# The norms' row of a random-feature layer goes through DRAM, and the first copies and the last blocks' steps are set anew

## The reference, cut to what matters

```python
def _rfs(xw, ab, AB, gs):
    dot_products = jnp.einsum('...d,rd->...r', xw, ab[:, None] * gs)
    correction = (0.5 * jnp.sum(xw * xw, axis=-1))[..., None] * (ab * ab)
    return 1.0 / math.sqrt(NUM_RFS) * AB * jnp.exp(dot_products - correction)
...
xn = _layernorm(x, axis=-1)
s = jnp.einsum('bsr,or->bso', _rfs(xn, ab, AB, proj), _rfs(input_weights, ab, AB, proj))
h = silu(tlin(xn, w1_w, w1_s)) * tlin(xn, w2_w, w2_s)
h = gelu(tlin(h, h1_w, h1_s))
h = gelu(tlin(h, h2_w, h2_s))
x = x + s * silu(tlin(h, w3_w, w3_s))
```

## Time and profile before

| | |
|---|---|
| median of 3 runs | 1345.27 us (1344.98 to 1350.56) |
| the profiled execution | 1345.51 us, of which the span from the first to the last instruction 1343.7 us |
| TensorE busy | 1320.0 us, 98% |
| mean granted TensorE clock | 0.997 |
| DMA moved | 193.85 MB, 144 GB/s on the mean |

### The profile page before, as it was taken

One profiled execution on the slowest core, in us unless ns is written; L12 is line 12 of the kernel. 1 busy time (PEld: TensorE's weight loads), 2 busy tenths in 40 slices (PEclk: granted clock), 3 DMA queues, 4 the chain that ended last, 5 costly groups with the idle time before them and its releaser, 6 DMA issues.

```text
span 1343.7 us, 16732 instructions
## 1 busy us (share of the span) xinstructions
PE 1320.0 (98%) x6428; PEld 1119.5 (83%) x6428; DVE 946.5 (70%) x1205; ACT 766.2 (57%) x1036; POOL 589.1 (44%) x596
## 2 busy tenths in 40 slices
PE   7989999999999999999999999999999999999997
PEld 6867898888988889888888888888898888988887
DVE  7767867778677786678865776656767567665665
ACT  5546655566555664466654666546565565655564
POOL 4556988999899998888880000000000000000000
PEclk9999999999999999999999999999999999999999
DMA  9798432545324552254521444224432244313351
GB/s 360 290 358 304 147 103 96 170 152 174 103 96 149 176 162 90 94 177 156 178 98 63 134 149 141 79 73 147 154 113 79 94 152 133 109 63 120 132 165 40
DMA packets 88372, 193.85 MB, mean 144 GB/s; under 512 B 10464, under 2 KB 12768, under 8 KB 87136
## 3 DMA queue, kind: packets, MB, share of 16 engines
q1 hardware_dynamic: 79520, 160.22, 35.9%
q0 software_dynamic: 8768, 32.51, 6.7%
HBM read 167.53 MB, written 34.60 MB: 150 GB/s over the span
## 4 chain that ended last, share of the span: by engine, by line
PE 92%; DMA 4%; POOL 2%; DVE 1%; issue 0%; ACT 0%; SPq 0%; POOLq 0%
PE ps L211 70%; PE ps L214 21%; DMA ring<-hs 2%; POOL ry L500 1%; DMA ry<-in_h 1%; PE ps L298 1%; DMA s<-in_h 1%; DMA quad<-in_w 1%; POOL quad L500 1%; DMA hs<-ry 0%; POOL s L500 0%; SPq L86 0%; DVE ry L194 0%; DVE split L194 0%; POOL hs L86 0%
## 5 line engine op out<-in xcount | busy, mean ns | idle before, releaser
L211 PE MATMUL ps<-split,ring 128*128 128x512 f32 x2800 | 766.2, 390 | 7.0 <-DMA ring<-hs 5.9
L211 PEld LDWEIGHTS ps<-split,ring 128*128 128x128 f32 x2800 | 526.4, 188 | 118.5 <-DMA ring<-hs 7.6
L194 DVE TENSOR_TENSOR split<-quad,split 128x1024 fp32r<-128x1024 f32 x258 | 338.1, 1319 | 197.4 <-ACT split L190 196.8
L190 ACT ACTIVATE split<-quad 128x1024 fp32r<-128x1024 f32 x258 | 267.1, 1052 | 74.2 <-PE ps L214 74.2
L214 PE MATMUL ps<-split,ring 128*128 128x512 f32 x784 | 305.2, 389 | 0.0
L211 PE MATMUL ps<-xT,w 128*128 128x512 f32 x768 | 216.4, 390 | 0.0
L544 POOL TENSOR_TENSOR cube<-cube,seen 128x256 f32<-128x256 f32 x176 | 194.5, 1105 | 13.8
L190 ACT ACTIVATE quad<-ps 128x512 f32<-128x512 f32 x192 | 114.7, 597 | 140.4 <-PE ps L214 140.4
L190 ACT ACTIVATE quad<-quad,cols 128x512 f32<-128x512 f32 (+1 forms) x194 | 139.0, 718 | 83.0 <-DVE quad L194 81.5
L194 DVE TENSOR_TENSOR quad<-quad 128x1024 f32<-128x1024 f32 x128 | 172.8, 1390 | 0.0
L214 PEld LDWEIGHTS ps<-split,ring 128*128 128x128 f32 x784 | 147.3, 188 | 30.5
(11 more groups left out here) (94 smaller groups left out, 1055.2 us busy)
## 6 DMA issues: line engine op xcount, KB each, us to landing
ring<-hs SPq DMA_DIRECT2D x448, 256.0 KB, 3.5
xin<-in_x SPq DMA_DIRECT2D x17, 512.0 KB, 5.7
s_h<-s SPq DMA_DIRECT2D x16, 512.0 KB, 2.6
seen<-in_h POOLq DMA_DIRECT2D x64, 128.0 KB, 3.6
ry<-in_x SPq DMA_DIRECT2D x15, 512.0 KB, 5.5
out<-ry SPq DMA_DIRECT2D x15, 512.0 KB, 2.6
hs<-in_h SPq DMA_DIRECT2D x4, 1024.0 KB, 19.7
ry<-in_h POOLq DMA_DIRECT2D x8, 512.0 KB, 9.5
```

Source lines behind the costliest of these rows:

```text
L190: return act.mark(lambda e: e.activation(dst, src, func, scale=scale))
L194: return dve.mark(lambda e: e.tensor_tensor(dst, a, b, op))
L211: pe.run(lambda e: e.matmul(dst, stat, mov, start=start, stop=stop, skip_group_check=loose))
```

## The change

The norms' row no longer goes over TensorE. `norms_out` stores the four columns of a half to a DRAM tensor `q_h` (512 single floats) from SP, after the norms; `norms_in` waits for that store and loads the row back into all 128 partitions of `qrow`. At a tile boundary both halves' `norms_out` stand in layer L1's last product, both `norms_in` in `between(2)`. DVE's norms wait for the store that read `sm[:, 3, :]` a tile earlier. The transposes of the second half use banks 6 and 7 instead of 7 and 4.

In the first tile SP sends the first norms' store, then copies only A11 and A12 of layer 0, loads the row, stores and loads the second half's, and only then issues the eight first feeds; w3's relayout comes after them, and w3's load between the two square layers. POOL copies A22 of layer 0 and A11 and A12 of layer 1 at the start of `factory_second`, A22 of layer 1 after two more loads. A21 is copied for neither layer.

The last four blocks' steps are interleaved: a block's scale and silu stand ahead of the gate and the add of the block before.

```diff
+        q_h = nc.dram_tensor("q_h", [NH, NB, P], F32).ap()
...
-                a = vv(q, mv[:, n0:n1, 1], y, ALU.mult, box["y"])
+                a = vv(q, mv[:, n0:n1, 1], y, ALU.mult, box["y"], *(q_stored[h % 2] for h in halves if q_stored[h % 2]))
...
-        def turn_norms(h, bank):
+        def norms_out(h):
+
+            sp.wait(norm_done[h]())
+            q_stored[h % 2] = d_qout[h % 2].send(sp, q_h[h].rearrange("b p -> p b"), sm[:, 3, 4 * (h % 2):4 * (h % 2) + 4], allow_slow_non_contiguous=True)
+
+        def norms_in(h):
 
             j = h % 2
-            pe.wait(norm_done[h](), *free[bank])
-            for b in range(NB):
-                i = 4 * j + b
-                tok = mm_mark(ps[:, bank, b * P:(b + 1) * P], sm[:, 3, i:i + 1].to_broadcast([P, P]), ident[:, :], True, True)
-            qrow_done[h] = cast(qrow[j][:, :], ps[:, bank, :], tok, *qrow_free[j])
-            free[bank] = [qrow_done[h]]
+            sp.wait(q_stored[j], *qrow_free[j])
+            qrow_done[h] = d_qin[j].send(sp, qrow[j], q_h[h].rearrange("b p -> (b p)").partition_broadcast(P))
...
-            sp.wait(*piece_stored[layer, k, p // 2 if p < Q else 2])
+            sp.wait(piece_stored[layer, k, name if p < Q else "sums"])
...
-        def copy_raw(lane, layer):
+        def copy_raw(lane, layer, names):
 
             src = wT[("h1", "h2")[layer]].rearrange("(j k p) (i c) -> j i k p c", j=2, p=P, i=2)
-            for j in range(2):
-                for i in range(2):
-                    copied[layer, j].send(lane, hs[layer][:, :, 2 * j + i, :], src[j, i])
+            for name in names:
+                p = PIECES.index(name)
+                tok = copied[layer, name].send(lane, hs[layer][:, :, p, :], src[p // 2, p % 2])
                 for k in range(Q):
-                    piece_stored[layer, k, j] = [copied[layer, j].token]
-
-        copy_raw(sp, 0)
-        d_w3d.send(sp, w3d.rearrange("p (k d) -> p k d", k=KH), w_kpm["w3"])
-        sp.wait(d_w3d.token)
-        d_w3.send(sp, w3[:, :, :].rearrange("p k d -> p (k d)").bitcast(F32), w3d)
+                    piece_stored[layer, k, name] = tok
...
             load(5)
             load(4)
-            copy_raw(pool, 1)
+            copy_raw(pool, 0, ["A22"])
+            copy_raw(pool, 1, ["A11", "A12"])
             make(4)
             make(5)
             load(6)
             load(7)
+            copy_raw(pool, 1, ["A22"])
             make(6)
             make(7)
...
-        for _ in range(RING):
-            feed()
...
-                side[3].append(lambda: turn_norms(0, 1))
+                norms_out(0)
+                copy_raw(sp, 0, ["A11", "A12"])
+                side[7].append(lambda: norms_in(0))
...
             if t == 0:
                 turn_rows(1, (0, 1))
-                turn_norms(1, 0)
+                norms_out(1)
...
+            if t == 0:
+                norms_in(1)
+                for _ in range(RING):
+                    feed()
             dots(h0, (4, 5), L0.at["v"])
...
                 factory_second()
+                d_w3d.send(sp, w3d.rearrange("p (k d) -> p k d", k=KH), w_kpm["w3"])
                 counted[0] = count_good()
...
+            def norms_away():
+                if t + 1 < NT:
+                    norms_out(h0 + 2)
+                    norms_out(h1 + 2)
...
+            if t == 0:
+                sp.wait(d_w3d.token)
+                d_w3.send(sp, w3[:, :, :].rearrange("p k d -> p (k d)").bitcast(F32), w3d)
             product_layer(L1, C, {
...
-                (6, 0): [split(C, "b22", 0, C.slot)], (6, 1): [split(C, "b22", 1, C.slot)], (6, 2): [fill, fill], (6, 3): [fill, fill, fill, fill]})
+                (6, 0): [split(C, "b22", 0, C.slot)], (6, 1): [split(C, "b22", 1, C.slot)], (6, 2): [fill, fill], (6, 3): [fill, fill, fill, fill, norms_away]})
...
                 if t + 1 < NT and n == 0:
                     turn_rows(h0 + 2, (4, 5))
-                    turn_norms(h0 + 2, 6)
                 if t + 1 < NT and n == 2:
-                    turn_rows(h1 + 2, (7, 4))
-                    turn_norms(h1 + 2, 5)
+                    turn_rows(h1 + 2, (6, 7))
                 if n == 2 and t + 1 < NT:
+                    norms_in(h0 + 2)
+                    norms_in(h1 + 2)
                     scale_y(h1)
...
-        for b in range(NB):
+        made_y = {}
+
+        def scaled(b):
             bank, col = y_place(h, b)
-            y = yt[:, b, :]
-            a = vv(y, ps[:, bank, col:col + D], w3s[:, 0, :], ALU.mult, y_done[h, b], *yt_free)
-            a = cast(y, y, a, func=ACT.Silu)
-            a = vv(y, y, s[0][:, b, :], ALU.mult, a, mixed[h])
-            a = vv(xin[0][:, b, :], xin[0][:, b, :], y, ALU.add, a, d_x[0].token)
+            a = vv(yt[:, b, :], ps[:, bank, col:col + D], w3s[:, 0, :], ALU.mult, y_done[h, b], *yt_free)
+            made_y[b] = cast(yt[:, b, :], yt[:, b, :], a, func=ACT.Silu)
+
+        def gated_y(b):
+            made_y[b] = vv(yt[:, b, :], yt[:, b, :], s[0][:, b, :], ALU.mult, made_y[b], mixed[h])
+
+        def added(b):
+            a = vv(xin[0][:, b, :], xin[0][:, b, :], yt[:, b, :], ALU.add, made_y[b], d_x[0].token)
             sp.wait(a)
             d_out.send(sp, o_h[h][:, b, :], xin[0][:, b, :])
 
+        for step, b in ((scaled, 0), (scaled, 1), (gated_y, 0), (added, 0), (scaled, 2), (gated_y, 1), (added, 1), (scaled, 3),
+                        (gated_y, 2), (added, 2), (gated_y, 3), (added, 3)):
+            step(b)
```

More of the change, by code:

```diff
@@ L82, in __init__, with send @@
         self.sem, self.count = sem, 0
-    def send(self, lane, dst, src):
+    def send(self, lane, dst, src, **how):
         self.count += 16
-        lane.todo.append(lambda e: e.dma_start(dst, src).then_inc(self.sem, 16))
+        lane.todo.append(lambda e: e.dma_start(dst, src, **how).then_inc(self.sem, 16))
         return self.sem, self.count
@@ L171, in build @@
         d_land = [port(f"d_land{i}") for i in range(5)]
-        copied = {(layer, j): port(f"copied{layer}{j}") for layer in range(2) for j in range(2)}
+        copied = {(layer, n): port(f"copied{layer}{n}") for layer in range(2) for n in ("A11", "A12", "A22")}
         stored = [port(f"stored{i}") for i in range(5)]
@@ L175, in build @@
         d_s = [port(f"d_s{j}") for j in range(2)]
+        d_qout, d_qin = [port(f"d_qout{j}") for j in range(2)], [port(f"d_qin{j}") for j in range(2)]
+        q_stored = [None, None]
         d_seen = [port(f"d_seen{i}") for i in range(2)]
@@ L509, in make @@
                 both(a12, a12, a11, ALU.subtract)
-                piece_stored[layer, k, 2] = [stored[use[n]].send(pool, hs[layer][k][:, Q:2 * Q, :], bufs[use[n]])]
+                piece_stored[layer, k, "sums"] = stored[use[n]].send(pool, hs[layer][k][:, Q:2 * Q, :], bufs[use[n]])
             pool.wait(*(v.token for v in d_w12))
```

## The result

The changed kernel took 1337.43 us in the median of 6 runs (1333.68 to 1338.84), the kernel before 1346.55 beside it (6 runs, 1344.9 to 1350.56). The ratio is 0.9924, with a 95% interval from 0.9903 to 0.9945: some 9 us faster, where 20 were forecast, and 5 us above the end of the range. The profiled execution took 1335.29, with a span of 1333.5.

The account below looks back on a forecast made before the run. It took TensorE, busy 98% of the span, as the bound, with transfers setting part of the first tile's time. Gains of 11.3 + 0.6 + 6.5 + 1.6 = 20.0 took 1345.5 to 1325.5 us, range 1321 to 1332.5.

Parts of the forecast that it names:

- The norms' row at the boundaries: Seven tile boundaries: fourteen slots of 0.81 us come off TensorE's path, 11.3 us gained.
- The cover: Boundaries: dots read the row over 40 us after the norms end, hiding store and load; priced at nothing.
- Banks 6 and 7: Next tile's first gated step shares these banks; spare time falls from 2.7 to 1.9 us, priced at nothing.
- slower rival: Each tile's first gated step waits for banks 6 and 7, seven times; 1358 at 4.7 us past the spare; chance 0.03.
- no release: Boundaries: removed slots uncover waits of the same length, and the first tile stays; 1343 us, chance 0.04.
- The end: Last four blocks: interleaved steps on DVE bring the last add forward, 1.6 us gained.
- The store of 512 single floats: Norms' store from SP, each half: lands in 3 to 6 us, priced at nothing.
- the element store is slow: First tile: two rows' stores hold SP, so the first feeds come after 63; 1338 us, chance 0.03.
- The copies and the first tile: First tile: fewer and moved copies bring sources and feeds sooner, 6.5 us gained, bounds 0 to 8.8.
- The clock's part: First tile, 91.0 to 102.1: clock rises from 0.85 to near 1.00; two thirds of 1.7 us counted.
- The ring waits: First tile: TensorE's waits for ring transfers shrink from 5.9 us to half a microsecond.
- The first tile's two rows: First tile: taking its two norms' rows off TensorE gains 0.6 us, bounds 0.3 to 1.1.

Follow-up runs that it names:

- c: Kernel before with only the change's copies, w3 and feeds; norms' rows on TensorE everywhere, old boundaries and end: 1344.6 us, ratio 0.9995.
- f: Changed kernel with each norms' store as 128 runs of 16 bytes to the same 2 KB, norms' right order left out: 1328.25 us, ratio 0.9865.
- g: Changed kernel with the 512 single floats stored 512 bytes apart and the row loaded from x: 1328.47 us, one run.
- k: Changed kernel with DVE transposing the norms before the store, which goes out as 16 runs of 128 bytes in 4 DMAs: 1328.94 us, ratio 0.9871.
- j: Changed kernel with the first tile's two rows on TensorE and POOL's first sums held until the second half's norms: 1329.97 us, ratio 0.9872.
- m: k with POOL's first three copies issued once the fourth source has landed, ahead of its sums: 1325.14 us, ratio 0.9836.
- a: Changed kernel with the first tile's two rows of norms on TensorE as before, all else as changed: 1337.28 us, ratio 0.9921.

## Why the prediction was wrong

**The norms' row at the boundaries, 11.3: right.** Seven boundaries, at the 1.67 of the six measured, gave 11.7 on the profiled execution, and the cleanest tile is 161.84 instead of 163.60. The runs bear it out: from the second tile's first gated matmul to the last add c, with the old boundaries and end, takes 1146.59, as the kernel before; the change takes 1134.91, f 1134.20, g 1134.21 and k 1134.24. No dots wait for the row. One tile lost 0.46 us of TensorE's time to no wait that the profile names (162.07 busy of 162.53), until 515.40, just as the store of its row ended; in f, g and k TensorE is full from 400 to 600. The cover was needed more than forecast: the row's load goes out 10.2 us after the store (340.53 to 350.73) and in the next tile 13.8 (501.64 to 515.40), and over 40 us of cover took both.

**Banks 6 and 7, nothing: right.** No bank wait shows at a boundary. The forecast's slower rival and *no release* both fall with the shorter tiles.

**The end, 1.6: right,** 1.69 to the last add. 1.1 came back behind it, in the last transfers; that was not followed further.

**The store of 512 single floats, priced at nothing: the step that failed.** The forecast put its landing at 3 to 6 us, from a mean of 0.097 us a packet on SP's queue. That mean is over packets of other transfers, each into its own stretch of memory. In the first tile the two stores landed after 14.6 and 18.8 us, and it was not SP's time that counted, but that beside the first one all other transfers together slowed down to 51 GB/s (14.0 to 23.4). With the same 2 KB in longer runs (f, k), or as many floats farther apart (g, one run), the time falls by 8.5 to 9.2 us in the medians; f and k were measured at other times than the change, and by their ratios to the kernel before beside them it is 7.1 to 7.9 (0.9924 less 0.9871 and 0.9865). In the first tile of the profiled executions the store cost 5.9 (f) to 6.4 us (k: second tile from 187.66) of the 9.2 that were missed there. The forecast had this as *the element store is slow*, at 1338, and gave it 0.03; its time was right to 1 us, but by a part of the wrong reason. It let the feeds come after 63; they left at 44.8, and the loss came through POOL's first source, which took 9.35 us longer beside the store, with the sums, copies and ring pieces behind it.

The rule of the Trainium skill that the forecast weighed, "DMA: Bandwidth & Descriptors", section Rules for kernel authors, one descriptor per element where the last dimension isn't contiguous, pointed the right way, and the packet row should not have outvoted it. The trace agrees with its count: f, with 128 runs a store instead of 512, has 83072 packets on SP's queue instead of 89216, and the difference is 16 stores x 384. But taken alone it would condemn g as well, where as many single floats land in 1.9 to 5.0 us: the measurement decides, and blames the crowded stretch.

**The copies and the first tile, 6.5: over-sized.** Alone (c) they give 1.5 in the medians, and that is not told apart from nothing. With a cheap store the second tile starts at 188.22 (f) and 187.66 (k), where the forecast's first tile and one boundary of 1.67 would put it at 184.9: 2.8 to 3.3 of the 9.2 are missing there still. The forecast followed the first source of delay, POOL's fourth load, rightly (52.1; forecast: by 53), and then let the burst behind it "start some 6 us sooner" as if that were only good. Sooner put it on the ring's next feed. The clock's part did not come: 1.00 instead of 0.85 in the stretch that was looked at, but lower in three others, as the result shows; in j and k it is 1.00 throughout. The ring waits stayed at 4 to 5 us in c, f, j and k, until m moved the copies.

**The first tile's two rows, 0.6:** j with them on TensorE and k with them through DRAM differ by 1.0, with overlapping runs: the size fits, and isn't shown.

What stays open: a and c have the same first tile by their code, but their first ring products start at 68.4 and 63.3. In c, DVE's last small step had begun at 22.99 and POOL started at 23.18; in a POOL was 0.1 us ahead of such a step. So small a lead could also be why runs of c (1343.1 to 1351.7) and of the kernel before (1344.2 to 1350.6) spread; that is argued, not shown.

## What to carry to other kernels

Price a scattered store by how many of its pieces land in the same small stretch, not by their number alone or by a queue's mean per packet, and look at GB/s beside the DMA share: here full engines that moved little were being held. A better clock in one stretch is no gain until the mean over the run says so. A transfer that is hidden for whoever waits for it can still cost everything else that uses the engines, so ask first what shares the stretch in which it runs. When a chain is made earlier, look up what its next burst will then meet, and move that as well.

## What the runs showed of the hardware

A store of 512 floats 4 bytes apart in 2 KB of DRAM landed after 14.6 us, and while it ran, from 14.0 to 23.4, the 16 DMA engines had a share of 0.97 and moved 51 GB/s; a second such store landed after 18.8, but beside it others moved at 400 to 414 GB/s for the first ten; as many floats 64 or 512 bytes apart landed in 5.5 and 5.0 us with 358 and 363 GB/s in the same stretch. POOL's elementwise sums beside DVE stretched some DVE steps on 128x4 floats from 0.15 us to 1.1 to 1.2, and two 128x256 normalising steps from 0.74 to 2.83 (j, a); the kernel before shows such normalising steps at 2.89 as well, beside POOL's first sums at 23.40. Keeping POOL idle for 3.1 us was worth 7.3, the clock's part included. In the changed kernel the slow store hid this: POOL started at 32.89, when DVE's statistics were done.
